# State space stage: the convolution as four diagonal products on TensorE, and a later place for some of ScalarE's work

## The reference, cut to what matters

```python
xz = h @ in_proj_w.T
x, z = jnp.split(xz, 2, axis=-1)              # 512 channels each
xpad = jnp.pad(x, ((0, 0), (3, 0), (0, 0)))
xc = conv_b
for k in range(4):
    xc = xc + xpad[:, k:k + L, :] * conv_w[:, k]
xc = silu(xc)
dt, Bm, Cm = split(xc @ x_proj_w.T, [16, 32])
dt = softplus(dt @ dt_proj_w.T + dt_proj_b)
# for each of 16 states n, along the sequence:
#   hst = exp(dt * A[:, n]) * hst + (dt * xc) * Bm[:, n];  y += hst * Cm[:, n]
y = (y + D * xc) * silu(z)
out = y @ out_proj_w.T
```

## Time and profile before

| | |
|---|---|
| median of 3 runs | 3355.52 us (3349.78 to 3358.53) |
| the profiled execution | 3378.07 us, its span 3376.3 us |
| granted TensorE clock over the span | 0.871 of 2.4 GHz |
| DVE busy over the span | 2045.4 us (61%) |
| state space stage, from its first scan to its last add | 1677.20 to 2828.68 us |

### The profile page before, as it was taken

One profiled execution on the slowest core, in us unless ns is written; L12 is line 12 of the kernel. 1 busy time (PEld: TensorE's weight loads), 2 busy tenths in 40 slices (PEclk: granted clock), 3 DMA queues, 4 the chain that ended last, 5 costly groups with the idle time before them and its releaser, 6 DMA issues. The chain is left out here.

```text
span 3376.3 us, 35979 instructions
## 1 busy us (share of the span) xinstructions
PE 2582.9 (76%) x11915; PEld 1782.3 (53%) x11946; DVE 2045.4 (61%) x3652; ACT 1050.8 (31%) x1621; POOL 1383.4 (41%) x865
## 2 busy tenths in 40 slices
PE   6555299945799999996276767767677665997998
PEld 2222166644799999996122333323233233665997
DVE  8999867554112211213898898989999895332211
ACT  4544122200111111111445554455454531221111
POOL 0000034425333333332058677686777862112332
PEclk8777699965899999998588888888888887998999
DMA  3000100010799999886200100100100000115996
GB/s 107 0 0 0 42 7 19 12 33 26 278 325 326 323 326 326 321 307 224 80 26 25 38 25 26 38 25 26 38 26 25 38 25 19 38 38 183 348 350 241
DMA packets 90562, 395.00 MB, mean 117 GB/s; under 512 B 20854, under 2 KB 48006, under 8 KB 63840
## 3 DMA queue, kind: packets, MB, share of 16 engines
q1 hardware_dynamic: 68864, 351.46, 29.4%
q0 software_dynamic: 21600, 42.37, 3.5%
HBM read 364.94 MB, written 39.29 MB: 120 GB/s over the span
## 5 line engine op out<-in xcount | busy, mean ns | idle before, releaser
L1236 POOL TENSOR_TENSOR ss_h<-ss_h,ss_cs 128x2048 f32<-128x2048 f32 x128 | 578.8, 4523 | 89.3 <-DVE ss_h L1589 81.4
L1310 PE MATMUL ss_y<-ss_h,all_ident 128*128 128x512 f32 x1024 | 528.7, 665 | 21.0 <-POOL ss_h L1236 14.1
L1092 DVE TENSOR_TENSOR experts_in<-experts_sil,experts_pU 128x512 f32<-128x512 f32 x176 | 121.0, 687 | 652.5 <-PE experts_pU L1036 611.2
L1589 DVE TENSOR_TENSOR_SCAN ss_h<-ss_da,ss_c_h,ss_dbu 128x512 f32<-128x512 f32 x384 | 470.8, 1268 | 44.3 <-ACT ss_da L1440 38.4
L1310 PEld LDWEIGHTS ss_y<-ss_h,all_ident 128*128 128x128 f32 x1024 | 220.5, 218 | 294.9 <-issue 278.0
L1440 ACT ACTIVATE ss_da<-ss_dt,ss_decay 128x512 f32<-128x512 f32 x512 | 326.5, 710 | 144.9 <-DVE ss_h L1589 86.9
L1036 PE MATMUL experts_pG<-experts_xt,experts_wa 128*128 128x128 f32 x2816 | 346.6, 277 | 0.4 <-DMA experts_wa<-in_w_all 0.3
L1036 PE MATMUL experts_pU<-experts_xt,experts_wa 128*128 128x128 f32 x2816 | 343.9, 275 | 0.0
L1045 PE MATMUL experts_pY<-experts_wa,experts_in 128*128 128x256 f32 x1408 | 332.7, 379 | 0.0
L1036 PEld LDWEIGHTS experts_pG<-experts_xt,experts_wa 128*128 128x128 f32 x2816 | 331.4, 193 | 1.4 <-DMA experts_wa<-in_w_all 0.6
L1582 DVE TENSOR_TENSOR ss_dbu<-ss_dtx,ss_bB 128x1024 f32<-128x1024 f32 x256 | 314.5, 1228 | 28.6 <-PE ss_bB L1300 1.3
(11 more groups left out here) (321 smaller groups left out, 3717.9 us busy)
## 6 DMA issues: line engine op xcount, KB each, us to landing
experts_wa<-in_w_all SPq DMA_DIRECT2D x176, 1536.0 KB
ss_cs<-ss_c_rows SPq DMA_DIRECT2D x32, 1024.0 KB, 4.6
moe_rows<-route_xn SPq DMA_DIRECT2D x16, 512.0 KB
all_x<-in_x SPq DMA_DIRECT2D x8, 512.0 KB, 9.3
gf_xb<-in_x SPq DMA_DIRECT2D x8, 512.0 KB, 3.8
ss_h<-moe_ys SPq DMA_DIRECT2D x4, 1024.0 KB, 7.0
moe_rows<-all_x SPq DMA_DIRECT2D x8, 512.0 KB, 3.3
experts_xr<-moe_rows,moe_token POOLq DMA_INDIRECT x176
```

What stands on the lines that cost most here:

```text
L1092: nc.vector.tensor_tensor(IN[t.two][:].rearrange("p f t -> p (f t)"), SIL[t.two][:], pU[t.two][:], ALU.mult)\
L1236: pool.tensor_tensor(h[:], h[:], CS[q % 2][:, n % GROUP].unsqueeze(1).to_broadcast([P, CI, BT]), ALU.mult)\
L1310: mm = pe.matmul(y[:, c], ident[:], H[n % RING][:, c], start=(n == 0), stop=(n == N - 1))
L1589: ins = V.tensor_tensor_scan(H[n % RING][:, c], DA[n % 2][:, c], DBU[:, c % 2], first, ALU.mult, ALU.add)
```

## The change

The convolution leaves DVE. ACT builds 16 diagonal matrices once (`TAP`, the identity times one tap's weights), and PE's new `convolve` multiplies four shifted views of `XR` by them, all summed in the bank that `x_part` wrote. ACT's second round becomes `copy_conv`: it reads that bank, adds the bias, and writes `XC`. It stands behind `decays` in its step, as `silu_x` does now. Two of the four `copy_dt` and two of the four `copy_z` move a step later or behind `decays`, `exponential` and `logarithm` one step later. To make room, `LN1` now lies in `XR`, and the second expert stage shares three index tiles with the first.

```diff
@@ state_space
+        TAP = m_.sb("tap", [P, CI, TAPS, P])
-        ZS, LN1 = m_.sb("zs", [P, CI, BT]), m_.sb("ln1", [P, CI, BT])
+        ZS, LN1 = m_.sb("zs", [P, CI, BT]), XR[:, :, TAPS - 1:]
@@ PE
                 def x_part(b, c):
                     ...
-                        wait(pe, "conv_done", b * CI + c)
+                        wait(pe, "xb_done", b * CI + c)
                     project(bank(b, c), WI, c * P, HT[b % 2], KD).then_inc(s["x_raw"], 1)
+                def convolve(b, c):
+                    wait(pe, "xr_done", b * CI + (c + 1))
+                    for t in range(TAPS):
+                        mm = pe.matmul(bank(b, c), TAP[:, c, t], XR[:, c, t:t + BT], start=(t == 0), stop=(t == TAPS - 1))
+                    mm.then_inc(s["conv_raw"], 1)
@@ PE out_part
-                            wait(pe, "conv_done", (b + 3) * CI)
+                            wait(pe, "xb_done", (b + 3) * CI)
@@ PE before the loop
-                wait(pe, "conv_done", CI)
+                wait(pe, "taps_done", 1)
+                for c in range(CI):
+                    convolve(0, c)
@@ PE loop, behind add_up
+                        if prep and n in (1, 2, 3, 4):
+                            convolve(b + 1, n - 1)
@@ ACT
+                for c in range(CI):
+                    for t in range(TAPS):
+                        tap = A_(TAP[:, c, t], ident[:], ACT.Copy, scale=conv_w[:, c, t:t + 1])
+                tap.then_inc(s["taps_done"], 1)
                 def copy_x(b, c):
                     wait(act, "x_raw", b * CI + (c + 1))
-                    q = bank(b, c)
-                    A_(XR[:, c, TAPS - 1:], q, ACT.Copy).then_inc(s["xr_done"], 1)
-                    wait(act, "xr_done", b * CI + (c + 1))
-                    A_(q, q, ACT.Identity, scale=conv_w[:, c, TAPS - 1:], bias=conv_b[:, c:c + 1]).then_inc(s["x_done"], 1)
+                    A_(XR[:, c, TAPS - 1:], bank(b, c), ACT.Copy).then_inc(s["xr_done"], 1)
+                def copy_conv(b, c):
+                    wait(act, "conv_raw", b * CI + (c + 1))
+                    wait(act, "skip_done", (b - 1) * CI)
+                    A_(XC[b % 2][:, c], bank(b, c), ACT.Identity, bias=conv_b[:, c:c + 1]).then_inc(s["xb_done"], 1)
@@ ACT loop
-                        if prep and n == 6:
-                            silu_x(b + 1)
                         if n < N - 1:
                             decays(b, n + 1)
+                        if prep and n in (2, 3, 4, 5):
+                            copy_conv(b + 1, n - 2)
+                        if prep and n == 6:
+                            silu_x(b + 1)
+                        if prep and n in (9, 10):
+                            copy_dt(b + 1, 2 * n - 17)
                         if prep and n in (8, 9):
                             copy_dt(b + 1, 2 * n - 16)
-                            copy_dt(b + 1, 2 * n - 15)
-                        if prep and n == 9:
+                        if prep and n == 10:
                             exponential(b + 1)
-                        if prep and n == 10:
+                        if prep and n == 11:
                             logarithm(b + 1)
@@ DVE loop
-                        if prep and n in (2, 3, 4, 5):
-                            convolve(b + 1, n - 2)
@@ build
+        r1 = Routing(nc, stack, "moe1", 16, 1, 2 * D, out, before=r0)
```

More of the change, by code:

```diff
@@ L608, with __init__ @@
 class Routing:
-    def __init__(self, nc, stack, tag, experts, k, width, out=None):
+    def __init__(self, nc, stack, tag, experts, k, width, out=None, before=None):
         m_ = Memory(nc, stack, tag)
@@ L618, in __init__ @@
         self.weight = m_.sb("weight", [P, NT, k])
-        self.expert = m_.sb("expert", [1, P], I32)
-        self.token, self.place = m_.sb("token", [P, P], I32), m_.sb("place", [P, P], I32)
+        if before is None:
+            self.expert = m_.sb("expert", [1, P], I32)
+            self.token, self.place = m_.sb("token", [P, P], I32), m_.sb("place", [P, P], I32)
+        else:
+            self.expert, self.token, self.place = before.expert, before.token, before.place
         self.direct = out is not None
@@ L1134, in state_space @@
         s = {n: m_.sem(n) for n in (
-            "loaded", "sel_steps", "decay_done", "pre", "stats_ready", "steps", "h_done", "t_raw", "ht_done", "x_raw", "x_done",
-            "z_raw", "z_done", "conv_done", "xc_done", "zs_done", "xp_raw", "bc1_done", "bc_done", "dt_raw", "u_done", "exp_done",
+            "loaded", "sel_steps", "decay_done", "pre", "stats_ready", "steps", "h_done", "t_raw", "ht_done", "x_raw",
+            "z_raw", "z_done", "taps_done", "conv_raw", "xb_done", "xc_done", "zs_done", "xp_raw", "bc1_done", "bc_done", "dt_raw", "u_done", "exp_done",
             "ln_done", "tail", "dt_done", "dtx_done", "spread", "da_done", "dbu_done", "scanned", "pr_done", "summed", "c_stored",
@@ L1394, in copy_x @@
                     wait(act, "x_raw", b * CI + (c + 1))
-                    q = bank(b, c)
-                    A_(XR[:, c, TAPS - 1:], q, ACT.Copy).then_inc(s["xr_done"], 1)
-                    wait(act, "xr_done", b * CI + (c + 1))
-                    A_(q, q, ACT.Identity, scale=conv_w[:, c, TAPS - 1:], bias=conv_b[:, c:c + 1]).then_inc(s["x_done"], 1)
+                    A_(XR[:, c, TAPS - 1:], bank(b, c), ACT.Copy).then_inc(s["xr_done"], 1)
[3 more added lines that the diff above has]
+                    A_(XC[b % 2][:, c], bank(b, c), ACT.Identity, bias=conv_b[:, c:c + 1]).then_inc(s["xb_done"], 1)
                 def silu_x(b):
-                    wait(act, "conv_done", b * CI + CI)
+                    wait(act, "xb_done", b * CI + CI)
                     A_(XC[b % 2][:], XC[b % 2][:], ACT.Silu).then_inc(s["xc_done"], 1)
@@ L1447, in _ @@
                     copy_x(0, c)
+                for c in range(CI):
+                    copy_conv(0, c)
                 silu_x(0)
@@ L1473, in _ @@
                             copy_ht(b + 1, 1)
+                        if prep and n in (2, 3, 4, 5):
[4 more added lines that the diff above has]
+                            copy_dt(b + 1, 2 * n - 17)
                         if prep and n in (8, 9):
                             copy_dt(b + 1, 2 * n - 16)
-                            copy_dt(b + 1, 2 * n - 15)
-                        if prep and n == 9:
+                        if prep and n == 10:
                             exponential(b + 1)
-                        if prep and n == 10:
+                        if prep and n == 11:
                             logarithm(b + 1)
+                        if n in (12, 13):
+                            copy_z(b, 2 * n - 23)
                         if n in (11, 12):
                             copy_z(b, 2 * n - 22)
-                            copy_z(b, 2 * n - 21)
                         if n == 13:
@@ L1492, in _ @@
                 pre = Chain(dve, s["pre"])
-                pre.link(V.memset(XR[:], 0.0))
+                pre.link(V.memset(XR[:, :, 0:TAPS - 1], 0.0))
                 def add_experts(b):
@@ L1539, in first_steps @@
                         V.tensor_tensor(DTX[0][:, part], u, XC[0][:, part], ALU.mult).then_inc(s["dtx_done"], 1)
[L1541 to L1553, removed]
+                PER = 2
                 def split_bc(b):
-                    ch = Chain(dve, s["steps"], b * PER + CI * (TAPS - 2))
+                    ch = Chain(dve, s["steps"], b * PER)
                     wait(dve, "bc1_done", b + 1)
@@ L1598, in _ @@
                 add_experts(2)
[L1599 to L1602, removed]
+                for b in range(3, NB):
+                    add_experts(b)
                 split_bc(0)
@@ L1631, in build @@
         X = m_.sb("x", [P, NT, D])
-        r0, r1 = Routing(nc, stack, "moe0", 64, 2, D), Routing(nc, stack, "moe1", 16, 1, 2 * D, out)
+        r0 = Routing(nc, stack, "moe0", 64, 2, D)
+        r1 = Routing(nc, stack, "moe1", 16, 1, 2 * D, out, before=r0)
         with ExitStack() as inner:
```

## The result

The changed kernel takes 3328.35 us (median of 4, 3326.05 to 3331.51), the kernel before 3356.15 us in the same comparison: ratio 0.9921, 95% interval 0.9904 to 0.9938, so 27.8 us less where 35.6 were forecast. A second comparison, on a chip where both are slower, gave 3342.68 against 3375.17, ratio 0.9902 (0.9888 to 0.9917), 32.5 us less.

A forecast was written before the change was run, and what follows sets the result against it. DVE bounds each block up to step 10's scans, POOL from there. 28.7 us from the convolution plus 8.45 from ACT's order less 1.5 in the prologue: 35.6 less, from 3355.5 to 3320 us, range 3296 to 3346.

The forecast's parts named there:

- DVE was nearly full, and the waits decide: Whole stage: DVE is busy 129.6 of 141 us a block, and its waits decide how much removed work pays.
- PE paces steps 2 to 5 at 9.6 us, with a round trip of 1.0: Steps 2 to 5: PE needs 9.6 us a step against DVE's 7.7, including 1.0 for copy_conv to free the bank.
- The term of 28.7 us: Gain in seven blocks from moving the convolution: 4.4 us in each of five, 3.3 in block 0, 3.4 in block 4.
- POOL sets the next block from step 10 on, so later gains do not count: From the end of step 10's scans POOL's 46.0 us stretch sets the next block; only earlier gains count.
- ScalarE's order, 8.45 us: Step 10 of seven blocks: with decays ahead of copy_dt, DVE's waits for decays vanish, 8.45 us in all.
- the walk: Step-by-step timing of block 2, also used for ACT's new order: DVE waits nowhere between step 8 and 15.
- The prologue, 1.5 us later: Ahead of the first scan: PE's 16 matmuls delay silu_x by 2.1 us; prologue 1.5 us later, between 0 and 2.1.
- The table load: Prologue, ahead of silu_x: 1.28 us by the row; the skill's 1.38 us drain would make the total 1.4 us higher.
- DVE did not get nearly all: Rival: PE keeps ahead in the steps, so DVE gains 58 + 8.45 us, total 3290; chance 13%.
- `copy_conv` never sat behind the decays: Rival: copy_conv waits behind decays, three steps each 1.3 to 2.56 us longer, total 3347 to 3374; chance 12%.
- PE's clock did not fall: Rival: PE at half clock in steps 2 to 4, 25 us a block more, total 3490; chance 8%.
- the point I gave: Steps 2 to 4: the half-clock rival decides from a PE step of 11.3 us on, a mean clock of 0.83.

The follow-up runs named there:

- layout_only: The kernel before with only the change's tiles (TAP allocated but unused, LN1 inside XR, index tiles shared): 3376.62 us, ratio 1.0002 to the kernel before.
- two_taps: The changed kernel with two of the four taps left out of each convolution in the loop (result incomplete): 3302.32 us, ratio 0.9829 to the kernel before.
- six_taps: The changed kernel with two extra matmuls, later overwritten, ahead of each convolution in the loop: 3374.60 us, ratio 1.0045 to the kernel before.
- order_only: The kernel before with only ScalarE's new order from step 6 on: 3374.33 us, ratio 0.9997 to the kernel before.
- low_on_dve: The changed kernel with the first half of low_part moved from POOL to DVE, in step 11: 3338.56 us, ratio 0.9890 to the kernel before.
- conv_only: The changed kernel with ScalarE's old order from step 6 on: 3354.38 us, ratio 0.9939 to the kernel before.
- read_ahead: The changed kernel with copy_conv directly behind copy_x, ahead of the step's decays: 3330.62 us, ratio 0.9925 to the kernel before.
- stats_first: The changed kernel with the statistics of the other 28 tiles on DVE ahead of split_bc(0): 3313.64 us, ratio 0.9867 to the kernel before.

## Why the prediction was right, and where it was off

*DVE was nearly full, and the waits decide.* Right. Of 68 us less work on DVE, 35 at most show in the stage.

*PE paces steps 2 to 5 at 9.6 us, with a round trip of 1.0.* Right, in mechanism and size: the step measured 9.63, `copy_conv` 0.69, the waits 1.15 and 2.06 (1.2 and 1.9 forecast), that of `add_out` 0.57 (0.7). The term of 28.7 us measured 27.3 in the first pair of profiles: 31.5 less in steps 2 to 5, 4.2 more in steps 6 and 7. Against layout_only's profile it is 25.1. two_taps and six_taps show that PE's work in these steps sets the pace: two matmuls less give 29 us back, two more cost 44.

*POOL sets the next block from step 10 on, so later gains do not count.* Right, shown by order_only and by low_on_dve. The period of block 2 to 3 came out at 138.3 us, where 140 was forecast; the periods of blocks 1 to 6 lie between 136.7 and 140.4. But the stretch from step 11 was not left alone, as the sum had it: it took 4.3 us less. Some 0.4 a block is a faster add on POOL (below), the rest is in block 1, where step 11 began late. That the first two profiles differ by 35.4 us in the stage, so near the 35.6 of the sum, is in this part luck.

*ScalarE's order, 8.45 us.* The mechanism is right: the waits for decays in step 10 are gone wherever the new order runs. The size is not: on its own (order_only) the order gave nothing that can be measured. I read the term off one profile, as if those seven waits belonged to the kernel. They sum to 8.45 us there, to 5.54 in a second profile of the same work (layout_only) and to 3.31 with the convolution's move alone. And I had found by the walk that DVE waits nowhere between step 8 and 15, where in fact it waits for `bB` at step 11 in some blocks, when PE is at low clock. Beside the convolution the term stays open: 1.2 us in steps 8 to 10 of the profiles, 11.7 us in the medians.

*The prologue, 1.5 us later.* 2.5 in the first pair, outside the 0 to 2.1 that I gave. `silu_x` came 1.85 us later, as reasoned, and `x_proj` took 6.30 us instead of less than 5.61, so that the rebate I had counted on did not come. In other profiles of the same prologue it took 5.40 us, and the prologue was 0.2 to 0.8 us longer than before. The place where 9 us lay was named, but not that a swap of two calls would fetch them.

*The table load.* The row decided rightly, 1.28 us and no drain on top: the ACTIVATE started 1.30 us after the load began (1615.41 to 1616.71).

*The rivals.* DVE did not get nearly all (two_taps shows what that would have been: 0.983). `copy_conv` never sat behind the decays. PE's clock did not fall but stood at 1.00 through 37.6 us of block 2 and at 0.97 to 1.00 in the same steps of the others. (Its price was added up wrongly: seven times 25 us, less the gain of 35.6, is some 140 and not 130.) And six_taps confirms the price of a slower PE: at a step of 11.3 us the gain is gone and 0.45% more, near the point I gave.

The chance of a gain was well placed and the size a little high: 27.8 and 32.5 us for 35.6. Against conv_only and order_only the sum fares less well: they came out at 20.8 us for 27 and at nothing for 8.

## What to carry to other kernels

Work taken from the fullest engine is worth what the engine that receives it can keep up with: write down both engines' length of a step, the lead between them, and the round trip of the buffer that they share, and walk a few steps. Then ask up to which point in the loop a gain counts; here a chain on another engine took over at step 10, and what was saved behind it only moved to the next block's first wait. And do not book a wait that comes and goes between blocks as a term of the kernel from one profile.

## What the runs showed of the hardware that was not expected

POOL's add of `dt` and the logarithm became faster when the logarithm's tile moved into `XR`, though it reads it with gaps: 2.16 us where it was 2.34, in the rows of before and of the changed kernel:

```profile
2104.85 2.34 POOL L1216 TENSOR_TENSOR ss_dt<-ss_dt,ss_ln 128x1024 f32<-128x1024 f32 x1
```

```profile
1925.67 2.16 POOL L1220 TENSOR_TENSOR ss_dt<-ss_dt,ss_xr 128x1024 f32<-128x1024 f32 x1
```

Two of these lie in each block's chain, 0.4 us; layout_only shows it as well (2.17 to 2.19 us, and 317.8 against 320.2 from step 11), and order_only, where the tile had not moved, does not (2.34 to 2.36). Why was not tried. The convolution's four shifted views of one tile cost PE nothing: 3.44 us from its first start to the next `spread` (1966.89 to 1970.33), as for `add_up` from an aligned tile. And PE's low clock after a pause lasted for different times in the same code. `x_proj` in the prologue stands behind 4.00 us of idle time in every profile with the new convolution. In the changed kernel's first profile it took 6.30 us, with a granted clock of 0.50 until near its end and 1.00 in its last microsecond. It took 6.28 in that of conv_only, and 5.40 in those of two_taps, six_taps, read_ahead, stats_first and low_on_dve. Before the change it took 5.61 behind 15.8 us of idle time. So the length of the pause did not decide how long the low clock lasted.
